# Gated activations of the feed-forward block kept for all six chunks, and two down projections issued later in their steps

## What is computed

```python
def reference(x, tok_W, tok_b, emb, qkv_w, o_w, w_gate, w_up, w_down):
    h = gelu(other @ W1 + readout @ W2 + b)          # "tok"
    h = h + attention(layernorm(h))                  # 16 heads of 64, bias per relative position
    h = h + ffn(layernorm(h))
    return h

def ffn(x):                                          # hidden width 768, integer weights / 127
    gate = x @ wg.T
    up   = x @ wu.T
    hid  = silu(gate) * up
    return hid @ wd.T
```

## Time and profile before

| | |
|---|---|
| timed runs | 2076.9, 2094.22, 2097.81 us (median 2094.22) |
| profiled execution, from first to last instruction | 2087.5 us, 46818 instructions |
| busy: PE, PEld, DVE, ACT, POOL | 91%, 83%, 83%, 70%, 42% |
| mean granted TensorE clock | 0.978 of 2.4 GHz |
| DMA | 17 GB/s, under 4% of the engines' time for any queue |

### The profile page before, as it was taken

How to read it: one execution, slowest core, us unless ns; L and a number is a source line. 1 busy time by engine, 2 the same in 40 slices (tenths; PEclk the granted TensorE clock), 3 DMA queues, 4 the chain that set the end, 5 groups by cost and what they waited for, 6 DMA issues and landing times.

```text
span 2087.5 us, 46818 instructions
## 1 busy us (share of the span) xinstructions
PE 1901.4 (91%) x15402; PEld 1723.9 (83%) x15402; DVE 1738.7 (83%) x5248; ACT 1463.5 (70%) x4034; POOL 881.6 (42%) x1103
## 2 busy tenths in 40 slices
PE   3799999998999989999999989999999999989995
PEld 1688888888888888888888888888888888878885
DVE  3489899888889879899788888889889788979884
ACT  5477677776777767677676767777677677767773
POOL 0244444444444434444444434434444444444441
PEclk9799999999999999999999999999999999999997
DMA  6000000000000000000000000000000000000000
GB/s 199 29 9 6 15 12 11 15 14 7 14 15 9 14 15 12 9 14 9 14 14 7 14 15 9 14 14 13 8 14 12 12 14 15 6 15 9 6 6 11
DMA packets 24925, 34.92 MB, mean 17 GB/s; under 512 B 2449, under 2 KB 17810, under 8 KB 24674
## 3 DMA queue, kind: packets, MB, share of 16 engines
q1 hardware_dynamic: 15202, 20.03, 3.2%
q10 hardware_dynamic: 8704, 8.36, 1.3%
q0 software_dynamic: 768, 3.21, 0.4%
HBM read 23.17 MB, written 8.42 MB: 15 GB/s over the span
## 4 chain that ended last, share of the span: by engine, by line
PE 54%; DVE 18%; ACT 16%; issue 9%; POOL 0%; DMA 0%; ACTq 0%; DVEq 0%; SPq 0%; POOLq 0%
PE ps L459 30%; PE ps L516 7%; PE ps L527 7%; PE ps L506 7%; ACT prob L699 5%; DVE prob L843 3%; PE ps L469 3%; DVE hT L886 3%; DVE pT L853 3%; DVE gate L877 2%; ACT L699 2%; ACT L675 2%; ACT qk L685 1%; ACT pT L706 1%; DVE heads L862 1%
## 5 line engine op out<-in xcount | busy, mean ns | idle before, releaser
L436 POOL TENSOR_TENSOR prob<-prob,inv 128x510 f32<-128x510 f32 x512 | 529.3, 1037 | 867.0 <-DVE inv L858 866.9
L699 ACT ACTIVATE prob<-prob,neg_top 128x255 f32<-128x255 f32 x1024 | 509.5, 502 | 53.2 <-DVE neg_top L843 52.7
L706 ACT ACTIVATE pT<-ps 128x512 fp32r<-128x512 f32 x512 | 277.9, 595 | 254.4 <-PE ps L516 254.3
L459 PE MATMUL ps<-xnT,wqk 128*128 128x256 f32 x3072 | 424.7, 287 | 1.4 <-DVE xnT L818 1.4
L843 DVE CUSTOM_DVE_ANT_0 prob<-ps,bias 128x255 f32<-128x255 f32 x1024 | 370.6, 418 | 17.6 <-PE ps L506 11.5
L459 PEld LDWEIGHTS ps<-xnT,wqk 128*128 128x128 f32 x3072 | 378.6, 189 | 2.5 <-DVE xnT L818 1.8
L853 DVE TENSOR_TENSOR pT<-ps,pT 128x512 fp32r<-128x512 f32 x512 | 328.3, 682 | 1.6 <-ACT pT L706 1.4
L516 PE MATMUL ps<-ident,prob 128*128 128x128 f32 x2048 | 280.8, 280 | 38.6 <-DVE heads L863 36.7
L527 PE MATMUL ps<-pT,v 128*128 128x256 f32 x2048 | 291.2, 285 | 0.3 <-DVE pT L853 0.3
L516 PEld LDWEIGHTS ps<-ident,prob 128*128 128x128 f32 x2048 | 220.8, 142 | 79.9 <-POOL prob L436 42.1
L527 PEld LDWEIGHTS ps<-pT,v 128*128 128x128 f32 x2048 | 267.9, 189 | 8.0 <-DVE pT L853 0.5
(11 more groups left out here) (89 smaller groups left out, 2645.5 us busy)
## 6 DMA issues: line engine op xcount, KB each, us to landing
xt<-x_cols SPq DMA_DIRECT2D x32, 256.0 KB, 2.6
r_rows<-readout_rows SPq DMA_DIRECT2D x32, 128.0 KB, 3.4
out<-h ACTq DMA_DIRECT2D x32, 128.0 KB
out<-h ACTq DMA_DIRECT2D x32, 127.0 KB
flipped<-bias_rows POOLq DMA_DIRECT2D x1, 3072.0 KB, 17.3
staged<-w_qk SPq DMA_DIRECT2D x8, 256.0 KB, 5.0
staged<-w_v SPq DMA_DIRECT2D x4, 256.0 KB, 8.6
staged<-w_o SPq DMA_DIRECT2D x4, 256.0 KB, 3.2
```

Source lines behind the costliest of these rows:

```text
L436: pool.tensor_tensor(pr, pr, by, ALU.mult).then_inc(prob_done, 1)
L459: mm = pe.matmul(dst, lhs(a, k), rhs(b, k), start=(start and n == 0), stop=(stop and n == last), skip_group_check=skip)
L699: ex = act.activation(pr, pr, ACT.Exp, bias=neg_top[:, g, hh, t:t + 1], scale=-1.0, accum_out=total[:, g, hh, t:t + 1])
L706: act.activation(pT[:, hh, 0].rearrange("p k q -> p (k q)"), ps[:, bank_t[hh], :], ACT.Copy).then_inc(pT_hi, 1)
```

## The change

`hT` is given room for six chunks (8 KB more in each SBUF partition), and its three users index it by m and not by m % 2. `down(2)` moves from the head of step 6 to the late part of step 6, ahead of `down(3)`; `down(4)` moves from the head of step 7 to the late part of step 7, ahead of `down(5)`. No instruction of DVE, ACT, POOL or SP moves, and the number of matmuls stays.

```diff
-        hT = sb("hT", [P, 2, 2, T], F32R)
+        hT = sb("hT", [P, MT, 2, T], F32R)
...
-                                      lambda a, k: hT[:, m % 2, a, t * P:(t + 1) * P],
+                                      lambda a, k: hT[:, m, a, t * P:(t + 1) * P],
...
                             norm_transposed(1, i - 1)
-                        if g == 6 and prev:
-                            down(i - 1, 2, has_lo)
                         if g in GU_EARLY and prev:
...
                             gate_up(i - 1, GU_EARLY[g], has_lo)
-                        if g == 7 and prev:
-                            down(i - 1, 4, has_lo)
                         if g == 7 and nxt:
...
                             if g == 6:
+                                down(i - 1, 2, has_lo)
                                 down(i - 1, 3, has_lo)
                                 gate_up(i - 1, 5, has_lo)
                             if g == 7:
+                                down(i - 1, 4, has_lo)
                                 down(i - 1, 5, has_lo)
...
-                    act.activation(hT[:, m % 2, 0, :], gated[:], ACT.Copy).then_inc(h_hi, 1)
+                    act.activation(hT[:, m, 0, :], gated[:], ACT.Copy).then_inc(h_hi, 1)
...
-                    dve.tensor_tensor(hT[:, m % 2, 1, :], gated[:], hT[:, m % 2, 0, :].bitcast(F32),
+                    dve.tensor_tensor(hT[:, m, 1, :], gated[:], hT[:, m, 0, :].bitcast(F32),
                                       ALU.subtract).then_inc(h_lo, 1)
```

## The result

The changed kernel takes 2099.99 us in the median of 14 runs (2098.19 to 2103.36), the kernel before 2088.9 us in 14 runs (2075.17 to 2097.81). The recorded ratio is 1.0064 with a 95% interval of 1.0045 to 1.0082 (the quotient of the two medians is 1.0053): slower, but by 11 us and not by the 29 forecast, and 2099.99 lies just under the range that was given (2101). The three runs shown ahead of the prediction lay high; over 14 runs the median before is 5 us lower. The range missed for both reasons together: 11 us on the old median of 2094.2 would have been 2105, and 29 us on the new one 2118, both inside it.

What follows compares the result with a forecast made beforehand. The bound was taken to change hands within an iteration, between DVE, PE and ACT. Two terms of +0.47 us make +0.94 us an iteration, 31 x 0.94 = 29.1 us, giving 2121 us (+1.3%), range 2101 to 2138.

Steps and rivals of the forecast that it cites:

- The two waits for `hT` go and DVE gives nothing for it: PE's waits ahead of down(2) (0.88 us) and down(4) (0.20 us) vanish; DVE, already busy, gets no earlier.
- the first rival: The waits go and nothing replaces them, as DVE runs ahead before add_bias(6): -33 us, 2061 us; chance 0.05.
- First term: Step 6: down(2) now comes behind PE's wait for biased and costs 4 matmuls there, +0.47 us an iteration.
- Second term: Step 7: norm_lo carries the earlier delay to queries_keys, and down(4) adds 4 matmuls late, +0.47 us an iteration.
- The second rival: Slack in steps 0 to 3 takes back what PE loses in step 7: no change, 2094 us; chance 0.06.
- the third (one term): Step 7: norm_lo does not carry the delay, so only 0.47 us is left: 2109 us; chance 0.10.
- TensorE's clock: New waits in steps 6 and 7 (0.68, 0.77 us, two under 0.5) too short to lower the clock; nothing counted.
- The fourth rival: The clock falls in step 6 or 7 once in each of 31 iterations: 42 us more, 2163 us; chance 0.03.
- I leave it as it is: At program and loop-pass starts, the wait for issue, 48.2 us in 15 places, was taken as unchanged.
- The level: Base for the whole kernel's time: 2123.3 us against the median 2094.2, 2118.7 against the three-run mean 2089.6; 2121 taken.

Runs made afterwards that it cites:

- the order that fills the same waits: Changed kernel, loop written out, down(2) behind gate_up(4), down(3) ahead of the wait for biased, down(4) behind the transposes: 2020.23 us.
- the written-out changed kernel: Changed kernel with the hardware loop replaced by 30 iterations in a row: 2052.49 us, against 2021.18 us for the kernel before written out.
- the padding: 32 always fulfilled PE waits ahead of gate_up(0) in each pass's first iteration: kernel before 2067.17 us (ratio 0.9947), changed kernel 2099.49 us (1.0099).

## Why the prediction was right in the body and wrong in the sum

- *The two waits for `hT` go and DVE gives nothing for it*: right. `gated` and `add_bias` take their place (0.71 and 0.54 us as the trace shows idle time; 0.77 was forecast for the second, and from start to start, with 0.70 us for the output projection as at 1059.35, PE loses 0.71 there), and the first rival (33 us faster) is excluded by the order that fills the same waits and gains 0.1 us an iteration.
- *First term, +0.47 us, `down(2)` behind the wait for `biased`*: right; 60.52 us with this move alone, and gone when the wait is put behind it (60.37 with both moves).
- *Second term, +0.47 us, `down(4)` late in step 7; DVE carries the first delay over `heads_added` and `norm_lo`*: right, 60.47 us alone, 60.94 with both. The second rival (what PE loses is taken back) and the third (one term) fall.
- *TensorE's clock*: at 1046 to 1052 in the changed kernel it did not fall, and in the written-out changed kernel, which has the same waits, it is at half level only within the first 106 us and the last 34. The Trainium skill ("TensorE: Matmul & The Clock Gate", the section on a second HAM failure mode) tells of a kernel whose short idle times between groups of matmuls make the clock go back and forth. This case's trace does not show that: idle times of 0.71, 0.54 and 0.34 us, three in 11 us, left the clock at 2.4 GHz. The fourth rival falls.
- *"I leave it as it is", of the iterations that begin a pass, and 31 x 0.94 = 29.1 us*: this is the step that failed. The prediction took the wait for issue at a loop start as a constant that the change leaves alone, and so put the full 0.94 us on the iterations that begin a pass too. These got 0.33 us shorter and not 0.95 longer: a difference of 1.28 us for each of 14, 17.9 us. Of the 1.24 us by which the gap shrank, 0.50 us is PE's last work hidden behind the fetch (2.87 to 2.37 us in starts with one fetch, and the same with `down(4)` alone), the rest is that 7 doubled fetches went (7 x 1.5 us over 14 starts is 0.75 us). The clock is not what did it: it fell at 9 of the 14 starts in both kernels, and that three of these falls lasted twice as long before is worth some 0.1 us a start. 31 x 0.95 - 17.9 = 11.6 us; the profiles differ by 10.7 us, the medians by 11.1.
- *The level*: the forecast was set on a median of three runs that later runs put 5 us lower. The profile was the better base: the changed kernel's profiled execution has a span of 2098.2 us for a time of 2100.05, so by the same 1.8 us that of before stands for 2089.3, close to the 2088.9 of 14 runs.

One thing stays open: why the fetch of the next piece, which the padding moves, falls beside that of the target in half of the passes of the kernel before and in none with `down(4)` moved. In 3 starts before and 10 after it is not seen at all. The padding shows that the place of the code matters, `down(4)` that the order at the end of the pass does, for it changes no count of instructions; how the two work together wasn't tried. And as each count is from one execution, how far it changes from run to run isn't known.

## What to carry to other kernels

Where two engines take turns as the bound, work moved off a visible wait only pays if nothing behind it waits for the busier engine; replay the list up to the next wait on that engine, and watch for a wait that stands ahead of work that doesn't need it. Replay a loop's start by itself: here PE's code for the next pass was fetched 1.17 us after the last wait in its list was fulfilled, 0.48 us of work that PE still had at that time was hidden in the fetch, and with some 2000 instructions of PE in a pass a start cost 4.65 us, so that writing the loop out was worth 3%, more than any order tried.

## What the runs showed of the hardware that I had not expected

- At a loop start 2.1 to 4.6 us pass from PE's last matmul to its next, and the gaps of 4.2 us and more are those in which two 16 KB packets of code are under way. Both the place of the code and the order at the end of the pass change how often that is. Some 16 instructions a pass that do nothing made the kernel before 0.5% faster (0.9947, 0.9922 to 0.9972).
- The clock at loop starts doesn't follow the length of the gap alone. In the changed kernel, after 1.99 us of idle time it fell for 750 to 753.4, and after the 2.05 us at 1000.75 it did not (busy times by stretch of the changed kernel; the column ahead of the last two is the granted clock, 0.52 for a stretch nearly all at 1.2 GHz, 1.00 for 2.4):

```profile
750.00:753.40 3.40, 3.40 (x18) 2.37 (x17) 0.69 (x1) 0.60 (x1) 0.45 (x1) 0.52 0.08 25
1000.00:1004.00 4.00, 3.25 (x25) 2.59 (x26) 1.08 (x2) 0.68 (x2) 1.14 (x2) 1.00 0.12 37
```

  In the changed kernel an iteration with such a fall takes 64.6 to 65.0 us and one without 63.4 to 63.6, so a fall costs about 1.3 us; it came at the same 9 of 14 starts in the changed kernel with padding, at 9 before, and at none in the profiled execution of the padded kernel before, whose gaps are longer (2.94 us on average). What decides at which starts it falls isn't shown. Nor is the clock the same in every run of a kernel, and the time goes with it: of the ten runs of the padded kernel before, 2060.98 us has a mean granted clock of 0.990 and 2072.75 us one of 0.982.
